# Three copies between statistics and aggregation taken out of VectorE's loop, and the aggregations moved

## The reference, cut to what matters

```
x = x + tanh(g_xattn[0]) * L0_xattn(ctx, ctx, layernorm(x))   # stage A feeds this
x = x + tanh(g_ffn[0])   * L0_ffn(layernorm(x))               # stage B
x = x + tanh(g_xattn[1]) * L1_xattn(layernorm(x), ctx)        # stage C
x = x + tanh(g_ffn[1])   * L1_ffn(layernorm(x))               # stage D

def layernorm(x, eps=1e-05):
    m = mean(x, axis=-1); v = var(x, axis=-1)
    return (x - m) / sqrt(v + eps)
```

## Time and profile before

| | |
|---|---|
| time, median of 3 runs | 2446.94 us (2446.25 to 2447.63) |
| span of the profiled execution, first to last instruction | 2442.8 us |
| PE busy | 2357.7 us, 97% |
| DVE busy | 2205.6 us, 90% |
| POOL busy | 1773.4 us, 73% |
| ACT busy | 1719.5 us, 70% |
| copies to ln_count, line 1491 | 256, 0.15 us each |

### The profile page before, as it was taken

The page is one execution under the profiler, slowest core; times in us unless marked ns, Lnnn a source line. Parts: engine busy times, 40 slices in busy tenths (PEclk is TensorE's granted clock), DMA queues, the critical chain, the costliest instruction groups (busy, mean ns, idle before and its releaser), DMA issues.

```text
span 2442.8 us, 70142 instructions
## 1 busy us (share of the span) xinstructions
PE 2357.7 (97%) x27814; PEld 2081.6 (85%) x27814; DVE 2205.6 (90%) x3678; ACT 1719.5 (70%) x3402; POOL 1773.4 (73%) x2512
## 2 busy tenths in 40 slices
PE   6899999999999999999999999999999999999897
PEld 5788888888888888888888888888888888888786
DVE  6879999999999999999999999999999999999963
ACT  4567777777777777777777777777777777777664
POOL 3667777777777777787777777777777777777653
PEclk9999999999999999999999999999999999999999
DMA  3000010010011010011001000001001001101000
GB/s 106 25 19 29 28 35 24 28 35 24 28 35 30 22 35 30 26 31 30 28 28 30 28 28 31 28 28 35 24 28 35 24 28 35 30 22 35 17 19 15
DMA packets 74326, 73.26 MB, mean 30 GB/s; under 512 B 6555, under 2 KB 73393, under 8 KB 74290
## 3 DMA queue, kind: packets, MB, share of 16 engines
q1 hardware_dynamic: 74290, 72.75, 9.5%
HBM read 54.90 MB, written 16.78 MB: 29 GB/s over the span
## 4 chain that ended last, share of the span: by engine, by line
PE 64%; DVE 19%; ACT 7%; POOL 7%; issue 2%; DMA 0%; POOLq 0%; SPq 0%; DVEq 0%; ACTq 0%
PE work L2136 13%; PE work L2137 11%; PE work L2138 11%; DVE m L1517 6%; PE scores L2229 6%; PE scores L2239 5%; PE work L2272 5%; PE work L2175 4%; DVE scores L1523 4%; ACT e L857 3%; POOL zt L417 3%; PE scores L2218 3%; ACT xn_D L814 3%; PE work L2153 2%; PE work L2159 2%
## 5 line engine op out<-in xcount | busy, mean ns | idle before, releaser
L857 ACT ACTIVATE e<-scores 120x1024 f32<-120x1024 f32 x512 | 513.4, 1029 | 88.3 <-PE scores L2239 56.6
L2136 PE MATMUL work<-xt_hi_B,w_hi 128*128 128x256 f32 x1536 | 456.5, 297 | 3.8 <-DVE y_lo_A L1497 1.6
L2137 PE MATMUL work<-xt_lo_B,w_hi 128*128 128x256 f32 x1536 | 430.2, 280 | 0.0
L2138 PE MATMUL work<-xt_hi_B,w_lo 128*128 128x256 f32 x1536 | 430.0, 280 | 0.0
L417 POOL TENSOR_TENSOR zt<-e 120x512 f32<-120x512 f32 x256 | 328.7, 1285 | 118.1 <-ACT e L857 112.1
L411 POOL TENSOR_TENSOR h_lo<-h_f,h_hi 128x256 fp32r<-128x256 f32 x384 | 279.5, 735 | 147.3 <-ACT h_hi L807 147.1
L1517 DVE TENSOR_REDUCE m<-scores 120x128 fp32r<-120x2048 f32 x128 | 291.0, 2273 | 66.2 <-PE scores L2229 66.0
L2136 PEld LDWEIGHTS work<-xt_hi_B,w_hi 128*128 128x128 f32 x1536 | 289.3, 188 | 60.6 <-DVE h_f L1511 24.9
L1523 DVE TENSOR_TENSOR scores<-scores,m 120x1024 f32<-120x1024 f32 x256 | 302.8, 1227 | 4.3
L1535 DVE TENSOR_TENSOR e<-e,work 120x2048 f32<-120x2048 f32 x128 | 291.4, 2277 | 0.2
L2137 PEld LDWEIGHTS work<-xt_lo_B,w_hi 128*128 128x128 f32 x1536 | 289.9, 189 | 0.0
(11 more groups left out here) (256 smaller groups left out, 7283.5 us busy)
## 6 DMA issues: line engine op xcount, KB each, us to landing
x_ln<-xp SPq DMA_DIRECT2D x64, 256.0 KB, 2.7
x_res<-xp SPq DMA_DIRECT2D x64, 256.0 KB, 2.7
y<-y_out SPq DMA_DIRECT2D x64, 256.0 KB, 2.2
ctx_f_A<-cp SPq DMA_DIRECT2D x64, 128.0 KB, 2.5
ctx_f_C<-cp SPq DMA_DIRECT2D x64, 128.0 KB, 2.0
qm<-mT SPq DMA_DIRECT2D x256, 4.0 KB
e<-wi SPq DMA_DIRECT2D x3, 768.0 KB, 5.5
w_ctx<-wc SPq DMA_DIRECT2D x1, 656.0 KB
```

Source lines behind the costliest of these rows:

```text
L857: return act.activation(e[0:SC, c, 2 * h:2 * h + 2, :, :].rearrange("p a b n -> p (a b n)"), scores[0:SC, 2 * h:2 * h + 2, :].rearrange("p ...
L2136: pe.matmul(out, a_hi, b_hi_, start=first, stop=False, skip_group_check=parts)
L2137: pe.matmul(out, a_hi, b_lo_, start=False, stop=False, skip_group_check=parts)
L2138: last = pe.matmul(out, a_lo, b_hi_, start=False, stop=end, skip_group_check=parts)
```

## The change

Inside VectorE's loop, stages A, B and C no longer call `moments`. Two new helpers do its parts without the copy: `sums` takes the two statistics, `mean_variance` the two aggregations. Stage D in the loop, and all stages before and behind the loop, keep `moments`.

- A: the statistics stay where they were. The wait for ln_mom_A stands at the residual x2, and the aggregation comes behind that residual.
- B and C: behind the statistics of B come the two statistics of C, the second with the wait for ln_mom_B; then the aggregation of B. The wait for ln_mom_C stands at key_max(0), behind which comes the aggregation of C.

```
+            def sums(st, x):
+                for i in range(NT):
+                    last = dve.bn_stats(stats[st][:, i, :], x[:, i, :])
+                return last
+
+            def mean_variance(st):
+                for i in range(NT):
+                    last = dve.bn_aggr(mv[st][:, i, :], stats[st][:, i, :])
+                return last
...
                 dve.wait_ge(s["ld_x_ln"], 16 * t)
-                moments("A", x_ln, t).then_inc(s["ln_eps_A"], 1)
+                sums("A", x_ln).then_inc(s["ln_mom_A"], 1)
                 dve.wait_ge(s["dn_mm"], nth(2, 6, t))
                 dve.wait_ge(s["x2_before"], t)
+                dve.wait_ge(s["ln_mom_A"], within(0, 1, t))
                 residual(x2, x1, W[2]).then_inc(s["res_B"], 1)
+                mean_variance("A").then_inc(s["ln_eps_A"], 1)
                 low(y_lo["A"][:, :, :], two(W[1], KC), y_hi["A"][:, :, :]).then_inc(s["yA_lo"], 1)
                 dve.wait_ge(s["M1_mm"], t)
                 key_max(1).then_inc(s["M1_max"], 1)
                 dve.wait_ge(s["woA_mm"], t)
                 residual(x1, x_res, W[2]).then_inc(s["res_A"], 1)
                 dve.wait_ge(s["res_A"], t)
-                moments("B", x1, t - 3).then_inc(s["ln_eps_B"], 1)
+                sums("B", x1).then_inc(s["ln_mom_B"], 1)
+                dve.bn_stats(stats["C"][:, 0, :], x2[:, 0, :])
+                dve.wait_ge(s["ln_mom_B"], within(0, 1, t - 3))
+                dve.bn_stats(stats["C"][:, 1, :], x2[:, 1, :]).then_inc(s["ln_mom_C"], 1)
+                mean_variance("B").then_inc(s["ln_eps_B"], 1)
                 dve.wait_ge(s["M0_mm"], t)
+                dve.wait_ge(s["ln_mom_C"], within(0, 1, t - 4))
                 key_max(0).then_inc(s["M0_max"], 1)
-                moments("C", x2, t - 4).then_inc(s["ln_eps_C"], 1)
+                mean_variance("C").then_inc(s["ln_eps_C"], 1)
                 values0_out(W[3]).then_inc(s["v0_pad"], 1)
```

## The result

The changed kernel takes 2480.97 us in the median of 4 runs (2478.85 to 2485.4), the kernel before 2446.6 in the runs beside it: a ratio of 1.0141, 95% interval 1.0128 to 1.0155, so 31 to 38 us more. Predicted were 2473.6 us, with a range of 2456 to 2490.

The account below looks back on a forecast made before the run. TensorE was taken as the bound, never idle after 1224.17 in a turn. Copies gained 0, late xn_B cost 0.46 us per turn: 58 x 0.46 = 26.7 us on 2446.94 gives 2473.6 us, range 2456 to 2490.

Parts of the forecast that it names:

- What bounds a turn: TensorE, never idle after 1224.17: a turn grows by what it is made to wait there; the 11.62 us D path stays.
- The wait for xn_B: Sign in the profile: TensorE idle before the transposes of B, 0.4 to 0.5 us, 58 times, released by ScalarE's xn_B.
- The copies at nothing: VectorE, stages A to C: copies and waits removed save 0.18 us per stage, covered by idle time; gain taken as 0.
- The rival on the faster side: VectorE from residual x1 to head_max(1): saved time counts in full, 2426 us or 2420 us; 8 in 100.
- A's aggregation, and what waits for it: Behind the residual x2: GpSimd's root A 1.05 us later, xt_lo_D and root B behind it 0.67 us later.
- B: C's statistics before B's aggregation: root B 0.67 us later, xn_B late, TensorE waits 0.46 us more per turn.
- both legs: Two paths to root B: GpSimd's queue frees at 1228.93, VectorE's mv_B is readable at 1228.88; both 0.67 us later.
- The size: TensorE's wait at xn_B: 0.46 us per turn, bounds 0.37 to 0.69, over 58 turns 26.7 us.
- the three waits at the residual x2: On VectorE, waits in front of the residual may add 0 to 0.1 us; taken as 0.
- the choice between load and matmul: TensorE's delay at the transposes of B: 0.52 us by the load, 0.42 by the matmul; 0.46 taken between.
- y_lo: On VectorE 0.16 us later, ending 1224.51 before TensorE's load at 1224.55: costs nothing, at most 0.1 us.
- The median against the profiled span: Median of the runs, 2446.94 us, lies 4.1 us above the profiled span; the 26.7 us are added to that median.

Follow-up runs that it names:

- e3: Kernel before with two copies of one column each instead of one in stages A, B and C of the loop: 2447.21 us, ratio 1.0001.
- e6: Kernel before with C's two statistics ahead of key_max(0) and C's copy gone, so M0_max comes late: 2447.3 us, ratio 1.0006.
- e2: Changed kernel with stages B and C put back as before, A's aggregation still behind the residual x2: 2476.09 us, ratio 1.0133.
- e8: Changed kernel with A's aggregation one instruction later still, behind y_lo_A: 2514.13 us, ratio 1.0278.
- e9: Kernel before with A changed, GpSimd's root A behind the second sum over heads, and x2_before the last wait at the residual: 2447.13 us, ratio 1.0000.
- e10: Changed kernel with one edit on GpSimd, root A behind the second sum over heads: 2473.32 us, ratio 1.0111.
- e7: Changed kernel with the three waits before the residual x2 reordered, x2_before last: 2474.18 us, ratio 1.0113.

## Why the prediction was right

*What bounds a turn.* Right: the turn grew by what TensorE was made to wait behind the transposes of D, and the 11.62 us in front of them stayed as they were. The wait for xn_B is there as foretold, 0.46 us for the loads; the turn, 36.90 us, came out above the 36.7 to 36.8 named.

*The copies at nothing.* Right, by e3 and e6: the time saved went into longer idle times before the residual x2 and before head_max(1). The rival on the faster side needed M0_max to be what TensorE waits for; e6 delayed it by 0.66 us at no cost. One reading there was too quick: the Trainium skill, VectorE: DVE Perf Modes, section The DRAIN you can't avoid, also says that a next operation that is not held starts earlier. With 0.07 us for a copy that lasts 0.15 us the trace agrees with that sentence. It does not agree with the section where a semaphore is said to cost nothing extra: the rows show 0.11 us.

*A's aggregation, and what waits for it.* Right in its path: root A late, GpSimd's idle time in front of xt_lo_D used up, root B late behind it (e2, e8, e9). Forecast was a root A 1.05 us later, and against the residual x2 it is just that (0.93 us behind its start, 1207.86 - 1206.93, where it was 0.12 ahead of it). Against the load of xn_D it is 1.13 us later, since the residual itself began 0.09 us later.

*B.* Right: both legs nearly alike. Alone, with A shifted, VectorE's puts the load of xn_B at 7.19 (e10) and GpSimd's at 7.28 (e2); in the changed kernel it is at 7.30. Forecast was a distance of 0.05 us between the legs, with GpSimd's the later one.

*The size.* Forecast 0.46 us per turn, measured 0.60, inside the stated bounds of 0.37 to 0.69. The term that was too small is that of the three waits at the residual x2: taken as 0 out of 0 to 0.1, it measured 0.09 (e7), and both legs hang on it. The rest is the choice between load and matmul: the transposes of B, started from idle, are at their next load after 0.59 us instead of 0.63 (1215.84 - 1215.25, and 1231.49 - 1230.86), so the gain from that is 0.04 us, not 0.06. With 0.52 + 0.09 - 0.04 the scores come 0.57 us later (0.56 by the rows). The other 0.04 us of the turn are no larger than what two executions differ by: e3 and e6 load the scores when the kernel before does, and their turns are 36.33 us. The forecast's 0.46 was a value chosen between 0.42 and 0.52 and not worked out; both of these lack the term of the waits.

*y_lo.* The margin of 0.04 us was indeed used up: the load of the product that needs it came 0.46 us after that of xn_D instead of 0.39. It cost nothing of its own, since TensorE waits later for xn_B in any case; the parallel paths did not add.

*The median against the profiled span.* The 4.1 us laid around the span were partly chance: the four runs of the changed kernel lie 1.9 to 2.4 us above their spans (the profiled one: 2485.4 and 2483.1). The forecast does not hang on them, for it adds 26.7 us to the median.

## What to carry to other kernels

Before an instruction is taken out or put off, follow its result to the engine that reads it and look at what stands in that engine's queue behind the reader: here four tiny operations of GpSimd, 1.1 us late, pushed three unrelated ones and then the one that TensorE needed. Two delays that meet at one instruction count as the larger, so undoing one may win back almost nothing; take each away alone and both together before calling one of them the cause. Busy time saved on an engine is worth nothing where it only lengthens that engine's next wait, as it did here on VectorE with its 90%.

## What the runs showed of the hardware that was not expected

The order of waits in front of one instruction had a price here. With the wait that ends last standing ahead of another wait whose threshold is computed, the residual started 0.09 us later (idle 0.88 against 0.79); over 58 turns the order of two lines was worth 5.8 us by the turns (58 x 0.10), 7.4 us by the losses in the table. Whether a wait with a constant threshold would have cost as much there was not tried.
